# Four head sums on column quarters of the matmul array, and an expert bias as a product with the identity (layer 0 of a four-layer kernel)

## What is computed

```
k = clip(k / sqrt(8)); q = clip(q / sqrt(8))
T1 = x;  T2 = 2 x x - 1;  ... T5 = 2 x T4 - T3
num[t] = sum_o beta_o * Tq_o[t] * cumsum_t(Tk_o * v)[t]              (per channel)
den[t] = sum_o beta_o * (sum_head Tq_o)[t] * cumsum_t(sum_head Tk_o)[t]
out    = (num / (den + 1e-7)) @ W_out
```

## Time and profile before

| | |
|---|---|
| device time, median of 3 | 2921.56 us |
| span of the profiled execution | 2983.9 us |
| PE busy, share of the span | 2684.1 us, 90% |
| DVE busy | 1941.2 us, 65% |
| layer 0, about | 0 to 325 us of the span |
| PE busy from 103.25 to 281.49 us | 171.39 of 178.24 us |

### The profile page before, as it was taken

The page is one execution under the profiler, slowest core; times in us unless marked ns, Lnnn a source line. Parts: engine busy times, 40 slices in busy tenths (PEclk is TensorE's granted clock), DMA queues, the critical chain, the costliest instruction groups (busy, mean ns, idle before and its releaser), DMA issues.

```text
span 2983.9 us, 40531 instructions
## 1 busy us (share of the span) xinstructions
PE 2684.1 (90%) x14378; PEld 1731.9 (58%) x14378; DVE 1941.2 (65%) x3806; ACT 1320.6 (44%) x3421; POOL 1239.8 (42%) x1116
## 2 busy tenths in 40 slices
PE   6899699999999999978879999999987988988888
PEld 3465245555555555544446666665546877766766
DVE  5778576877877777647657777776665272646633
ACT  4454424334344344344446666664542223355442
POOL 2553067677677677734542333320001340333331
PEclk8899799999999999989999999999977776889898
DMA  4453200000000000028012222211002211212113
GB/s 164 137 181 113 98 1 1 1 1 1 1 1 1 1 1 1 1 92 214 31 49 56 65 69 67 69 52 41 8 32 94 68 57 43 60 29 65 33 47 92
DMA packets 172520, 159.55 MB, mean 53 GB/s; under 512 B 98736, under 2 KB 149168, under 8 KB 171504
## 3 DMA queue, kind: packets, MB, share of 16 engines
q1 hardware_dynamic: 149536, 90.92, 10.9%
q0 software_dynamic: 22784, 66.05, 7.2%
HBM read 127.16 MB, written 59.51 MB: 63 GB/s over the span
## 4 chain that ended last, share of the span: by engine, by line
PE 42%; DVE 7%; ACT 3%; issue 2%; another core or an unknown queue 1%; DMA 0%; POOL 0%; SPq 0%; POOLq 0%; DVEq 0%; ACTq 0%
PE bank L65 37%; PE bank L2053 4%; DVE work L2009 1%; DVE work L3289 1%; ACT L3231 1%; DVE work L3071 0%; ACT weights_odd L2937 0%; DVE work L3337 0%; DVE work L1986 0%; DVE weights_odd L3339 0%; DVE weights_odd L3337 0%; DVE work L3488 0%; PE bank L2884 0%; DVE weights_even L3289 0%
## 5 line engine op out<-in xcount | busy, mean ns | idle before, releaser
L1492 POOL TENSOR_TENSOR work<-work 128x512 f32<-128x512 f32 x384 | 494.8, 1289 | 305.6 <-DVE work L1484 285.4
L65 PE MATMUL bank<-work 64*128 64x256 f32 (+5 forms) x4384 | 588.2, 351 | 23.4 <-DVE work L3488 7.2
L65 PE MATMUL bank<-weights_odd,normed_channels 128*128 128x512 f32 (+3 forms) x1152 | 520.4, 561 | 52.7 <-DVE work L1484 52.0
L65 PEld LDWEIGHTS bank<-work 64*128 64x128 f32 (+4 forms) x4384 | 412.4, 171 | 225.1 <-issue 144.7
L1484 DVE TENSOR_TENSOR work<-bank,work 128x512 f32<-128x512 f32 x360 | 244.4, 685 | 104.2 <-PE bank L65 100.3
L2023 ACT ACTIVATE work<-bank,work 128x256 f32<-128x256 f32 x512 | 236.0, 472 | 156.3 <-DVE work L2009 145.9
L65 PEld LDWEIGHTS bank<-weights_odd,normed_channels 128*128 128x128 f32 x1152 | 187.4, 198 | 183.2 <-DVE work L1484 94.2
L2009 DVE TENSOR_REDUCE work<-bank 128x2 f32<-128x512 f32 x256 | 165.3, 685 | 172.3 <-PE bank L65 151.5
L595 POOL DMA_INDIRECT weights_even<-in_L_Wx,expert_slots x112 | 111.6, 996 | 355.6 <-PE bank L668 270.9
L1559 ACT ACTIVATE work<-bank,work 128x256 f32<-128x256 f32 x256 | 119.0, 470 | 290.1 <-DVE work L1546 289.9
L65 PE MATMUL bank<-work,weights_odd 128*128 128x512 f32 (+3 forms) x520 | 209.3, 518 | 34.3 <-ACT work L3253 9.0
(11 more groups left out here) (343 smaller groups left out, 4633.6 us busy)
## 6 DMA issues: line engine op xcount, KB each, us to landing
filter_matrices<-in_L_filters SPq DMA_DIRECT2D x24, 512.0 KB, 8.1
work<-filter_matrices SPq DMA_DIRECT2D x16, 768.0 KB
weights_even<-noted_rows SPq DMA_DIRECT2D x56, 132.0 KB
noted_rows<-in_empty SPq DMA_DIRECT2D x11, 660.0 KB, 10.3
noted_rows_in<-in_empty SPq DMA_DIRECT2D x8, 660.0 KB, 10.2
weights_odd<-noted_rows_in SPq DMA_DIRECT2D x40, 132.0 KB
work<-token_rows SPq DMA_DIRECT2D x16, 256.0 KB, 3.0
token_rows_out<-in_zeros SPq DMA_DIRECT2D x6, 640.0 KB, 20.1
```

Source lines behind the costliest of these rows:

```text
L65: return pe.matmul(out, lhsT, rhs, start=first, stop=last, skip_group_check=True)
L1492: gp.tensor_tensor(self.sum_of(p), self.sum_of(p), self.product_of(p), ALU.add).then_inc(s["l1_add"], 1)
```

## The change

The ten head sums become twelve matmuls. Orders 1 to 4 each use one matrix of 128 x 32 and write to one quarter of the partitions (`o * 32`), so that four matmuls lie side by side on four column quarters of the array. They are issued in one burst at offset 7 (`tensor_first_sums`), no longer one order per offset. Order 5 follows at offset 8 (`tensor_last_sums`) by batch element: the columns of batch element `j` go to quarter `j`, with a matrix whose ones stand in the upper 16 of the 32 columns. `vector_keys` works on all 128 partitions instead of 80, and `head_back` has 128 rows with the weights of the orders at their new places. Waits on `l0_sums` count 4 per group instead of 10. The constants of layer 0 shrink from 784 to 448 words a partition. The bias matmul takes the identity (128 x 128) and all 128 rows of the bias.

```diff
@@ tensor_down
-                mm(pe, out, ones, W[0:1, 2 * F + self.nf:2 * F + self.nf + P], last=False)
+                mm(pe, out, self.k.ident, W[:, 2 * F + self.nf:2 * F + self.nf + P], last=False)
@@ layer0_constants
-    sums = np.zeros((P, L0_ORDERS, L0_ROWS), np.float32)
+    sums = np.zeros((P, 2, L0_TILE), np.float32)
     back = np.zeros((P, P), np.float32)
-    for o in range(L0_ORDERS):
-        for h in range(L0_HEADS):
-            sums[h * L0_DH:(h + 1) * L0_DH, o, o * L0_HEADS + h] = 1.0
-            back[o * L0_HEADS + h, h * L0_DH:(h + 1) * L0_DH] = beta[o + 1]
+    last = L0_ORDERS - 1
+    for h in range(L0_HEADS):
+        channels = slice(h * L0_DH, (h + 1) * L0_DH)
+        sums[channels, 0, h] = 1.0
+        sums[channels, 1, L0_HEADS + h] = 1.0
+        for o in range(last):
+            back[o * L0_TILE + h, channels] = beta[o + 1]
+        for j in range(BPG):
+            back[j * L0_TILE + L0_HEADS + h, channels] = beta[last + 1]
@@ tensor_attention
-                on.wait_ge(s["l0_kc"], g)
-                for i in range(2):
-                    self.order_ready(on, g, o, i)
-                    mm(pe, self.sums[i][0:L0_ROWS, :], self.head_sum[:, o, :], self.T[o][i], first=o == 0,
-                       last=o == L0_ORDERS - 1).then_inc(s["l0_sums"], 1)
+                if o == L0_ORDERS - 2:
+                    self.tensor_first_sums(pe, on, g)
+                if o == L0_ORDERS - 1:
+                    self.tensor_last_sums(pe, on, g)
                 yield
+    def tensor_first_sums(self, pe, on, g):
+        s = self.k.sem
+        on.wait_ge(s["l0_kc"], g)
+        for i in range(2):
+            for o in range(L0_ORDERS - 1):
+                self.order_ready(on, g, o, i)
+                last = mm(pe, self.sums[i][o * L0_TILE:(o + 1) * L0_TILE, :], self.head_sum, self.T[o][i], last=o >= BPG)
+            last.then_inc(s["l0_sums"], 1)
+    def tensor_last_sums(self, pe, on, g):
+        s, o = self.k.sem, L0_ORDERS - 1
+        for i in range(2):
+            self.order_ready(on, g, o, i)
+            for j in range(BPG):
+                c = slice(j * SEQ, (j + 1) * SEQ)
+                last = mm(pe, self.sums[i][j * L0_TILE:(j + 1) * L0_TILE, c], self.head_sum_last, self.T[o][i][:, c], first=False)
+            last.then_inc(s["l0_sums"], 1)
@@ vector_keys
-        on.wait_ge(s["l0_sums"], 10 * g + 10)
+        on.wait_ge(s["l0_sums"], 4 * g + 4)
...
-            v.tensor_tensor_scan(self.kc[0:L0_ROWS, c], self.ones[0:L0_ROWS, :], self.sums[1][0:L0_ROWS, c], 0.0,
-                                 ALU.mult, ALU.add).then_inc(s["l0_kc_scan"], 1)
+            v.tensor_tensor_scan(self.kc[:, c], self.ones, self.sums[1][:, c], 0.0, ALU.mult, ALU.add).then_inc(s["l0_kc_scan"], 1)
```

More of the change, by code:

```diff
@@ L683, in tensor_down @@
     def tensor_down(self, pe, on, m):
-        F, ones = self.nf * P, self.k.ones[0:1, :]
+        F = self.nf * P
         if not self.one:
@@ L829 @@
 L0_FF = 4
-L0_ROWS = L0_ORDERS * L0_HEADS
-L0_CONST = L0_ORDERS * L0_ROWS + P + SEQ
+L0_TILE = 32
+L0_CONST = 2 * L0_TILE + P + SEQ
 def chebyshev_weights():
@@ L864, in __init__ @@
         self.consts = take(L0_CONST)
-        at = L0_ORDERS * L0_ROWS
-        self.head_sum = self.consts[:, 0:at].rearrange("p (o r) -> p o r", o=L0_ORDERS)
-        self.head_back = self.consts[0:L0_ROWS, at:at + P]
+        at = 2 * L0_TILE
+        self.head_sum, self.head_sum_last = self.consts[:, 0:L0_TILE], self.consts[:, L0_TILE:at]
+        self.head_back = self.consts[:, at:at + P]
         self.ones = self.consts[:, at + P:at + P + SEQ]
@@ L927, in tensor_attention @@
                 on.wait_ge(s["l0_attended"], g - 1)
-                mm(pe, self.ends[:, :], self.head_back, self.kc[0:L0_ROWS, :]).then_inc(s["l0_den"], 1)
+                mm(pe, self.ends[:, :], self.head_back, self.kc).then_inc(s["l0_den"], 1)
             yield
@@ L950, in scalar_attention @@
                 on.wait_ge(s["l0_proj"], 3 * g + i + 1)
-                on.wait_ge(s["l0_sums"], 10 * g)
+                on.wait_ge(s["l0_sums"], 4 * g)
                 on.wait_ge(s["l0_key_value"], 5 * g)
@@ L1028, in vector_odd @@
                 self.counted(on, "l0_even", self.EVEN, g, ("twice", i))
-                on.wait_ge(s["l0_sums"], 10 * (g - 1) + 6)
+                on.wait_ge(s["l0_sums"], 4 * (g - 1) + 2)
                 op = v.tensor_tensor(T[2][i], T[0][i], self.twice[i], ALU.mult)
@@ L1078, in vector_keys @@
             c = slice(j * SEQ, (j + 1) * SEQ)
-            v.tensor_tensor_scan(self.kc[0:L0_ROWS, c], self.ones[0:L0_ROWS, :], self.sums[1][0:L0_ROWS, c], 0.0,
-                                 ALU.mult, ALU.add).then_inc(s["l0_kc_scan"], 1)
+            v.tensor_tensor_scan(self.kc[:, c], self.ones, self.sums[1][:, c], 0.0, ALU.mult, ALU.add).then_inc(s["l0_kc_scan"], 1)
         on.wait_ge(s["l0_kc_scan"], 2 * g + 2)
-        kc = self.kc[0:L0_ROWS, :]
-        v.tensor_tensor(kc, kc, self.sums[0][0:L0_ROWS, :], ALU.mult).then_inc(s["l0_kc"], 1)
+        v.tensor_tensor(self.kc, self.kc, self.sums[0][:, :], ALU.mult).then_inc(s["l0_kc"], 1)
     def vector_route(self, v, on):
```

## The result

The changed kernel takes 2891.2 us (median of four, 2887.7 to 2897.74); the kernel before, beside it, 2922.07 (median of four). These two medians are 30.9 us apart, a ratio of 0.9894. The ratio on record isn't their quotient; it is 0.9883, 95% interval 0.9865 to 0.9901: 29 to 39 us less, 34 at the middle. The forecast of 2900 us, 21.5 us less, had the sign and most of the mechanism, but the gain was about half as large again.

What follows compares the result with a forecast made beforehand. PE bounds five periods of layer 0 (178.2 us); afterwards DVE's 134.8 + 6.5 + 9.8 = 151, 27 less. Minus 5 for the clock gives 22, scaled to 21.5: 2921.6 - 21.5 = 2900 us, range 2889 to 2915.

Steps and rivals of the forecast that it cites:

- PE bounds the five periods: Layer 0, five periods between DVE's reciprocals, 103.25 to 281.49 us: PE busy 171.4 of 178.2 us, DVE 134.8.
- The sums cost 2.9 us instead of 8.6: Head sums in layer 0: matmuls on four quarters run together, 5.7 us less PE work a group, 28.5 in five periods.
- The bias saves 0.35 us a half: Bias matmul in each half of a down step: 128 rows save 0.35 us, over 40 halves 14 us of PE work.
- PE's work falls to 128.9 us, below DVE: Five periods of layer 0: PE's work falls from 171.4 to 128.9 us, below DVE's 134.8.
- The handovers keep 6.5 us, line 1079's wait goes, 9.8 us stay: DVE's waits in five periods: next-group handovers 6.5 instead of 19.1 us, head sums' 14.8 gone, DMA and values 9.8 stay.
- Five microseconds off for the clock and the coupling: Five periods: 5 us off the 27 us gain, for PE's clock falling from 0.97 to about 0.92 and coupling with DVE.
- Nothing outside the stretch: Layer 0's first period (71 to 103 us) and last (281 to 315 us) keep their lengths within 1 us.
- DVE becomes the bound: Five periods of layer 0: DVE leads, and the time is its 134.8 us plus what it still waits for, 151 us.
- (a): Rival, head sums: streams don't run together at 512 columns, sums stay 8.6 us, only the bias pays; 14 us, 2907; chance 0.05.
- (b): Rival, five periods: PE's lower clock gives most of it back; 2 to 12 us gained, 2914; chance 0.13.
- (d): Rival, five periods: slower, PE's clock falls for whole periods; at clock 0.70 10 us more, 2931; chance 0.05.
- (c): Rival, expert weight gathers in layer 0: they come late and PE waits for them; 2916 to 2922 us; chance 0.07.

Runs made afterwards that it cites:

- the repeat: The changed kernel run again without further edits, in the third set of runs: ratio 0.9916, five periods of layer 0 in 149.2 us.
- the move alone: Kernel before, with ten unpacked sums and old bias, but orders 1 to 4 in one burst at offset 7: ratio 1.001 (0.9999 to 1.0022).

## Why the prediction was right or wrong

- *PE bounds the five periods.* Right: the bias alone took 16.2 us off PE's work and 16.2 off the stretch, and taking 13.6 us from DVE in the kernel before shortened the stretch by 2.2.
- *The sums cost 2.9 us instead of 8.6.* Right: 2.84. Eight matmuls of 0.86 us in 1.85 are 3.7 times, slightly more than the 3.5 of the row of layer 3 (3.5 over 1.01, which the prediction has as 3.4). The trace doesn't agree with the 3.07 times that the Trainium skill (TensorE: Matmul & The Clock Gate, "Measured speedup vs the span model") gives for four row tiles.
- *The bias saves 0.35 us a half.* Nearly: 0.39, so 16 us of PE work instead of 14.
- *PE's work falls to 128.9 us, below DVE.* 130.9 and 134.1.
- *The handovers keep 6.5 us, line 1079's wait goes, 9.8 us stay.* 6.7, gone, and 7.2 with line 1085's 0.8: 13.9 in all instead of 16.3. The waits for rows were 7.0 and are 5.1; why they are shorter was not tested.
- *Five microseconds off for the clock and the coupling.* This is the step that failed, and it holds most of the miss: the forecast has a stretch of 156 us, the terms without the deduction say 151, measured were 147.8. The other 3 us are the smaller waits (2.4) and DVE's work (0.7). The deduction rested on a clock that falls from 0.97 to 0.92; the stretch kept 0.96, and 0.95 in the repeat, which is 1.4 us longer. The clock does fall in single periods, as in this one of the repeat, 1.5 us longer than those with four pair steps at 1.00:

```profile
191.80:221.91 30.11, 26.98 (x195) 22.04 (x194) 26.90 (x49) 19.89 (x60) 19.19 (x18) 0.94 0.65 204
```

But that is 1 to 3 us over five periods. In the first and the last period it fell from 0.82 to 0.71 and from 0.85 to 0.70, and no time was lost there, where DVE is busy for 26.4 of 29.8 and 33.0 of 34.0 us. A small term beside it, to scale 22 us down to 21.5 because the times are 2.1% shorter than the span, had no ground either: that difference lies in layers 2 and 3.
- *Nothing outside the stretch.* 2.1 us came in the first period, from a pair's rows. The bias alone leaves that wait as it was and the move alone shortens it, so it seems to go with the place of the sums; this was not tested further.
- *DVE becomes the bound.* Half right: it led the four-pair periods only, level with a second chain, and with five pairs PE led. That the sum came out near is in part luck: in it DVE's busy time and its waits were added up, and that sum is the length whichever engine leads.

So the gain in layer 0 was 32 us, where the terms without the deduction say 27 (the stretch alone: 30.4, and 29.1 with the repeat's). Of the rivals, (a) is excluded by the burst's 1.85 us, (b) by the clock of 0.96, (d) by the result. (c) is seen in its beginnings: PE waits 1.7 us for weights, for which it had no wait in the stretch before, at a DMA share of 0.62.

## What to carry to other kernels

Where TensorE leads, matmuls with 32 or fewer useful output rows are worth packing on column quarters, also in fp32 and with 512 moving columns: here eight took 1.85 us, where two one by one take 1.72. Work the gain out per stage: the leading engine's work shrinks until the next engine's work plus the waits that stay is longer. Take nothing off for the clock in a round sum: here 5 us were most of the miss. To learn whether an engine leads, change its work both ways and read single periods: with four pair steps less DVE work moved nothing and more moved all of it, and either run alone would have misled.

## What the hardware showed that I had not expected

A matmul with one row of contraction between full-height ones cost 0.42 us, against 0.22 for a full-height one in its place (179.60 to 179.82 us): the smaller product is the dearer one. Matmuls on different quarters overlapped whatever their order in the program, also where the q and the k sum of one quarter are neighbours (1.87 us for the burst): a matmul that has to wait for its own quarter didn't hold up those behind it for other quarters. The same kernel differed by 57 to 68 us between sets of runs (2925 against 2982 and 2993), two of which name the same chip; in the profiles the difference lies in layer 2 (814 against 852 to 861 us) and layer 3 (784 to 791 against 803 to 817).
